# A Fourier basis of a quarter period, enc x spectrum in fp32r parts, and the mixing of tile 0 behind four sums

## The reference, cut to what matters

```python
base = jnp.einsum('bsd,od->bso', x, W_base) + b_base
e0 = jnp.einsum('bsd,rd->bsr', x, enc0)            # rank 32
e1 = jnp.einsum('bsd,rd->bsr', x, enc1)            # rank 8
w0 = coefs0 * mask0; w1 = coefs1 * mask1           # 3 experts
decoded = einsum('bsr,eor->ebso', e0, w0) + einsum('bsr,eor->ebso', e1, w1)
update = real_fourier_orthogonal_multiply(decoded).sum(axis=0)
return base + update * SCALING                     # SCALING = 0.5
...
x = x + L0_ffn(L0_cond(x, itok_B_0_15, L0_cond_weights), ...)
x = x + L1_ffn(L1_cond(x, itok_B_0_30, L1_cond_weights), ...)
```

## Time and profile before

| | us |
|---|---|
| median of 3 runs | 227.8 |
| lowest and highest | 227.55 and 227.83 |
| the profiled execution's own time | 227.68 |
| its span, first to last instruction | 225.5 |

### The profile page before, as it was taken

The page is one execution under the profiler, slowest core; times in us unless marked ns, Lnnn a source line. Parts: engine busy times, 40 slices in busy tenths (PEclk is TensorE's granted clock), DMA queues, the critical chain, the costliest instruction groups (busy, mean ns, idle before and its releaser), DMA issues.

```text
span 225.5 us, 3597 instructions
## 1 busy us (share of the span) xinstructions
PE 220.1 (98%) x1212; PEld 185.2 (82%) x1212; DVE 98.8 (44%) x147; ACT 75.0 (33%) x199; POOL 110.1 (49%) x133
## 2 busy tenths in 40 slices
PE   7799999999999999999999999999999999999995
PEld 2568888888888888888888888888888888888884
DVE  4246444344544343445443444454434444544334
ACT  2067233333322333333223333332233333322211
POOL 4757754355566545445665454456654544522200
PEclk9999999999999999999999999999999999999999
DMA  6931022333222323322233323221232332212112
GB/s 201 310 99 52 9 96 96 102 93 84 72 53 96 99 96 99 99 63 88 52 96 99 96 99 99 71 81 52 96 99 96 99 99 81 73 49 90 47 49 93
DMA packets 13543, 20.42 MB, mean 91 GB/s; under 512 B 2618, under 2 KB 4538, under 8 KB 13538
## 3 DMA queue, kind: packets, MB, share of 16 engines
q1 hardware_dynamic: 10642, 18.16, 25.3%
q0 software_dynamic: 2048, 1.05, 2.4%
q10 hardware_dynamic: 848, 1.14, 1.5%
HBM read 11.96 MB, written 8.39 MB: 90 GB/s over the span
## 4 chain that ended last, share of the span: by engine, by line
PE 95%; DMA 3%; DVE 0%; ACTq 0%; issue 0%
PE f_ps L443 26%; PE y_ps L423 26%; PE f_ps L453 13%; PE f_ps L460 13%; PE f_ps L465 13%; DMA basis_sb<-in_fourier_basis 3%; PE a_ps L481 2%; PE a_ps L408 1%; PE y_ps L417 0%; DVE x L392 0%; PE a_ps L460 0%; PE f_ps L417 0%; PE a_ps L465 0%; ACTq L260 0%; ACTq L259 0%
## 5 line engine op out<-in xcount | busy, mean ns | idle before, releaser
L224 POOL TENSOR_TENSOR x<-x_in,bias 128x512 f32<-128x512 f32 x32 | 40.9, 1278 | 81.0 <-issue 46.9
L217 POOL DMA_INDIRECT gathered<-in_L_cond_weights,row_now x58 | 56.5, 974 | 13.2 <-issue 10.1
L443 PE MATMUL f_ps<-a_high,y_high 128*128 128x512 f32 x128 | 53.8, 420 | 0.0
L443 PE MATMUL f_ps<-a_low,y_high 128*128 128x512 f32 x128 | 50.3, 393 | 0.0
L358 DVE TENSOR_TENSOR x<-f_ps,x 128x512 f32<-128x512 f32 x32 | 22.1, 692 | 49.4 <-PE f_ps L443 47.9
L286 ACT ACTIVATE y_high<-y_ps 128x512 fp32r<-128x512 f32 x32 | 19.1, 597 | 69.6 <-PE y_ps L423 69.6
L282 ACT ACTIVATE y_high<-y_ps 128x512 fp32r<-128x512 f32 x32 | 19.1, 597 | 61.4 <-PE y_ps L423 61.4
L460 PE MATMUL f_ps<-b_sign,y_high 128*128 128x512 f32 x124 | 36.5, 415 | 0.0
L423 PEld LDWEIGHTS y_ps<-blocks,x_in 128*128 128x128 f32 x256 | 33.5, 191 | 3.5 <-issue 0.7
L423 PEld LDWEIGHTS y_ps<-blocks,x 128*128 128x128 f32 x256 | 33.4, 191 | 3.2 <-DVE x L358 0.5
L453 PE MATMUL f_ps<-a_high,y_low 128*128 128x512 f32 x128 | 35.1, 396 | 0.0
(11 more groups left out here) (44 smaller groups left out, 73.0 us busy)
## 6 DMA issues: line engine op xcount, KB each, us to landing
x_in<-in_x SPq DMA_DIRECT2D x31, 256.0 KB, 2.7
out_x<-x SPq DMA_DIRECT2D x31, 256.0 KB, 2.0
gathered<-in_L_cond_weights,row_now POOLq DMA_INDIRECT x58, 2.4
w_sb<-in_L_ffn_W_base SPq DMA_DIRECT2D x1, 512.0 KB, 7.5
w_sb<-in_L_ffn_W_base ACTq DMA_DIRECT2D x1, 512.0 KB, 8.9
basis_sb<-in_fourier_basis SPq DMA_DIRECT2D x1, 257.0 KB, 3.3
basis_sb<-in_fourier_basis ACTq DMA_DIRECT2D x1, 257.0 KB, 6.7
bias<-in_L_ffn_b_base SPq DMA_DIRECT2D x1, 256.0 KB
```

The lines of the kernel that those rows point to most:

```text
L217: nc.gpsimd.indirect_dma_start(gathered[:, slot, layer, :], None, mix_rows[layer], IndirectOffsetOnAxis(rows[:, layer:layer + 1].bitcast(u ...
L224: nc.gpsimd.tensor_tensor(out=x1[:, slot, :], in0=x_in[:, slot, :], in1=bias[:, :], op=ALU.add).then_inc(biased, 1)
L443: last = nc.tensor.matmul(f0_ps[:, :], y0_high[:, k * P:(k + 1) * P], a[:, k, :], start=(k == 0 and a is a_high), stop=(k == CHUNKS - 1 an ...
```

## The change

It does four things.

1. The table holds a quarter of a period (129 columns) in one array of 258 KB instead of two of 257 KB, and only SP loads it. `decode` gets two copies of the 40 ranks side by side (rows 0 to 39 and 64 to 103) and two negated chunks. PE forms four sums of two fp32 matmuls of 129 columns each instead of two sums of two with 257; the second sum of sines waits for the negated chunks. DVE builds `spectrum` from four quarters, some of them read backwards.
2. enc is loaded twice, to partitions 0 to 39 and 64 to 103, from ACT's queue instead of SP's. ACT rounds it to fp32r (`enc_parts`), DVE puts the rest into rows 64 and up. `spectrum` is split into `spectrum_high` and `spectrum_low` too. Per bank one fp32r matmul takes both parts of enc with the high spectrum, and a second one takes enc's high part (64 rows) with the low spectrum, in place of one fp32 matmul.
3. The masks are issued first on ACT's queue, and DVE treats them before `row_of` and before clearing `blocks`.
4. The mixing of tile 0 stands behind all four banks on PE, its `expand` and y0_high behind all four a_high on ACT, and low0(1) behind all a_low on DVE, where the signs are converted before the residual of tile 0. There are 13 warm-up matmuls instead of 18.

The diff, without declarations of semaphores and with shape changes left out:

```diff
+        decode = sb("decode", [P, CHUNKS + 2, 2, ENC_LOW], f32)
         enc_sb = sb("enc_sb", [P, T], f32)
-        odd_part = sb("odd_part", [P, HALF], f32)
-        mirrored = sb("mirrored", [P, HALF], f32)
+        enc_parts = sb("enc_parts", [P, T], f32r)
         constant2 = sb("constant2", [P, 1], f32)
+        sines = sb("sines", [P, 2, QUARTER], f32)
         spectrum = sb("spectrum", [P, T], f32)
+        spectrum_high = sb("spectrum_high", [P, T], f32r)
+        spectrum_low = sb("spectrum_low", [P, T], f32r)
...
+        sine_ps = [sums[:, 0:QUARTER] for sums in (y1_ps, y0_ps)]
+        cosine_ps = [sums[:, 0:QUARTER] for sums in (f1_ps, f0_ps)]
...
-            sp.dma_start(coefs_sb[:, :, :], coefs).then_inc(coefs_loaded, 16)
-            sp.dma_start(basis_sb[:, 1], basis[1]).then_inc(basis_loaded[1], 16)
+            sp.dma_start(coefs_sb[:, :, :, :], coefs).then_inc(coefs_loaded, 16)
+            sp.dma_start(basis_sb[:, :, :], basis).then_inc(basis_loaded, 16)
             load_w(sp, 0)
-            sp.wait_ge(enc_zero, 1)
-            sp.dma_start(enc_sb[0:R, :], enc).then_inc(enc_loaded, 16)
             sp.dma_start(bias[:, :], b_base.partition_broadcast(P)).then_inc(bias_loaded, 16)
...
+            act.dma_start(masks_sb[:, :, :, :], masks).then_inc(masks_loaded, 16)
             act.dma_start(kinds[:, :, :], kinds_in).then_inc(kinds_loaded, 16)
-            act.dma_start(masks_sb[:, :, :], masks).then_inc(masks_loaded, 16)
-            act.dma_start(basis_sb[:, 0], basis[0]).then_inc(basis_loaded[0], 16)
+            act.wait_ge(enc_zero, 1)
+            for first in (0, ENC_LOW):
+                act.dma_start(enc_sb[first:first + R, :], enc).then_inc(enc_loaded, 16)
             load_w(act, 1)
             act.dma_start(x_in[:, 0, :], x_tiles[0]).then_inc(x_loaded[0], 16)
...
-            act.wait_ge(odd_done, 1)
-            nc.scalar.activation(odd_part[:, :], odd_ps, ACT.Copy, scale=SCALING).then_inc(odd_ready, 1)
-            act.wait_ge(blocks_zero, 1)
-            expand(0, 0)
+            def spectrum_side(half):
+                act.wait_ge(quarters_ready, 2 * half + 2)
+                nc.scalar.activation(spectrum_high[:, halves[half]], spectrum[:, halves[half]], ACT.Copy, scale=SCALING
+                                     ).then_inc(spectrum_high_ready, 1)
+            for n in range(2):
+                act.wait_ge(sines_done, n + 1)
+                nc.scalar.activation(sines[:, n, :], sine_ps[n], ACT.Copy).then_inc(sines_ready, 1)
+            act.wait_ge(enc_loaded, 32)
+            nc.scalar.activation(enc_parts[:, :], enc_sb[:, :], ACT.Copy).then_inc(enc_high_ready, 1)
+            spectrum_side(0)
+            spectrum_side(1)
             def high0(count):
                 act.wait_ge(mixed0, count)
                 nc.scalar.activation(y0_high[:, :], y0_ps[:, :], ACT.Copy).then_inc(y0_high_ready, 1)
...
             for k in range(CHUNKS):
-                if k == FIRST_MIX:
-                    high0(1)
                 act.wait_ge(a_done, k + 1)
                 nc.scalar.activation(a_high[:, k, :], a_ps[k][:, :], ACT.Copy).then_inc(a_high_ready, 1)
+            act.wait_ge(blocks_zero, 1)
+            expand(0, 0)
+            high0(1)
             expand(1, 0)
...
-            nc.vector.memset(blocks[:, :, :, :], 0.0).then_inc(blocks_zero, 1)
-            nc.vector.memset(decode[:, :, :], 0.0).then_inc(decode_zero, 1)
+            nc.vector.memset(decode[:, :, :, :], 0.0).then_inc(decode_zero, 1)
             dve.wait_ge(partition_ready, 1)
             nc.vector.tensor_scalar(channel[:, :], partition[:, :], C - 1, None, ALU.bitwise_and).then_inc(channel_ready, 1)
+            dve.wait_ge(coefs_loaded, 16)
+            dve.wait_ge(masks_loaded, 16)
+            nc.vector.tensor_tensor(out=masked[:, :, :, :], in0=coefs_sb[:, :, :, :], in1=masks_sb[:, :, :, :], op=ALU.mult).then_inc(masked_ready, 1)
+            dve.wait_ge(masked_ready, 1)
+            nc.vector.tensor_tensor(out=pair[:, :, :], in0=masked[:, 0, :, :], in1=masked[:, 1, :, :], op=ALU.add).then_inc(pair_ready, 1)
+            dve.wait_ge(pair_ready, 1)
+            dve.wait_ge(decode_zero, 1)
+            for copy in range(2):
+                nc.vector.tensor_tensor(out=decode[:, 0:CHUNKS, copy, 0:R], in0=pair[:, :, :], in1=masked[:, 2, :, :], op=ALU.add).then_inc(decode_ready, 1)
+            dve.wait_ge(decode_ready, 2)
+            nc.vector.tensor_scalar(decode[:, CHUNKS:, :, 0:R], decode[:, 1:3, :, 0:R], -1.0, None, ALU.mult).then_inc(negated, 1)
             dve.wait_ge(channel_ready, 1)
             dve.wait_ge(kinds_loaded, 16)
             nc.vector.tensor_scalar(row_of[:, :, :], kinds[:, :, :], float(C), channel[:, :], ALU.mult, ALU.add).then_inc(row_of_ready, 1)
-            dve.wait_ge(coefs_loaded, 16)
-            dve.wait_ge(masks_loaded, 16)
-            nc.vector.tensor_tensor(out=masked[:, :, :], in0=coefs_sb[:, :, :], in1=masks_sb[:, :, :], op=ALU.mult).then_inc(masked_ready, 1)
-            dve.wait_ge(masked_ready, 1)
-            nc.vector.tensor_tensor(out=pair[:, :], in0=masked[:, 0, :], in1=masked[:, 1, :], op=ALU.add).then_inc(pair_ready, 1)
-            dve.wait_ge(pair_ready, 1)
-            dve.wait_ge(decode_zero, 1)
-            for first, rank, at in ((0, R0, 0), (CHUNKS * R0, R1, R0)):
-                part = slice(first, first + CHUNKS * rank)
-                nc.vector.tensor_tensor(out=decode[:, :, at:at + rank], in0=pair[:, part].rearrange("p (q r) -> p q r", r=rank),
-                                        in1=masked[:, 2, part].rearrange("p (q r) -> p q r", r=rank), op=ALU.add).then_inc(decode_ready, 1)
-            dve.wait_ge(odd_ready, 1)
-            nc.vector.tensor_scalar(constant2[:, :], odd_part[:, 0:1], 2.0, None, ALU.mult).then_inc(constant_ready, 1)
+            nc.vector.memset(blocks[:, :, :, :], 0.0).then_inc(blocks_zero, 1)
+            dve.wait_ge(sines_ready, 1)
+            nc.vector.tensor_scalar(constant2[:, :], sines[:, 0, 0:1], 2.0, None, ALU.mult).then_inc(constant_ready, 1)
             dve.wait_ge(constant_ready, 1)
-            nc.vector.tensor_scalar(mirrored[:, :], odd_part[:, :], -1.0, constant2[:, :], ALU.mult, ALU.add).then_inc(mirrored_ready, 1)
-            dve.wait_ge(mirrored_ready, 1)
-            dve.wait_ge(even_done, 1)
-            nc.vector.scalar_tensor_tensor(out=spectrum[:, 0:HALF], in0=even_ps, scalar=SCALING, in1=odd_part[:, :],
-                                           op0=ALU.mult, op1=ALU.add).then_inc(spectrum_ready, 1)
-            nc.vector.scalar_tensor_tensor(out=spectrum[:, T - 1:HALF - 1:-1], in0=even_ps[:, 1:HALF - 1], scalar=SCALING,
-                                           in1=mirrored[:, 1:HALF - 1], op0=ALU.mult, op1=ALU.add).then_inc(spectrum_ready, 1)
+            dve.wait_ge(cosines_done, 1)
+            nc.vector.tensor_tensor(out=spectrum[:, 0:QUARTER], in0=cosine_ps[0], in1=sines[:, 0, :], op=ALU.add).then_inc(quarters_ready, 1)
+            dve.wait_ge(cosines_done, 2)
+            dve.wait_ge(sines_ready, 2)
+            nc.vector.scalar_tensor_tensor(out=spectrum[:, HALF:QUARTER - 1:-1], in0=cosine_ps[1][:, 0:QUARTER - 1], scalar=constant2[:, :],
+                                           in1=sines[:, 1, 0:QUARTER - 1], op0=ALU.add, op1=ALU.subtract).then_inc(quarters_ready, 1)
+            nc.vector.tensor_tensor(out=spectrum[:, HALF + 1:HALF + QUARTER], in0=cosine_ps[1][:, 1:QUARTER], in1=sines[:, 1, 1:QUARTER],
+                                    op=ALU.add).then_inc(quarters_ready, 1)
+            nc.vector.scalar_tensor_tensor(out=spectrum[:, T - 1:HALF + QUARTER - 1:-1], in0=cosine_ps[0][:, 1:QUARTER - 1], scalar=constant2[:, :],
+                                           in1=sines[:, 0, 1:QUARTER - 1], op0=ALU.add, op1=ALU.subtract).then_inc(quarters_ready, 1)
+            dve.wait_ge(enc_high_ready, 1)
+            nc.vector.tensor_tensor(out=enc_parts[ENC_LOW:, :], in0=enc_sb[ENC_LOW:, :], in1=enc_parts[ENC_LOW:, :].bitcast(f32),
+                                    op=ALU.subtract).then_inc(enc_low_ready, 1)
+            for half, columns in enumerate(halves):
+                dve.wait_ge(spectrum_high_ready, half + 1)
+                nc.vector.scalar_tensor_tensor(out=spectrum_low[:, columns], in0=spectrum[:, columns], scalar=SCALING,
+                                               in1=spectrum_high[:, columns].bitcast(f32), op0=ALU.mult, op1=ALU.subtract
+                                               ).then_inc(spectrum_low_ready, 1)
...
             for k in range(CHUNKS):
-                if k == FIRST_MIX:
-                    low0(1)
                 dve.wait_ge(a_high_ready, k + 1)
                 nc.vector.tensor_tensor(out=a_low[:, k, :], in0=a_ps[k][:, :], in1=a_high[:, k, :].bitcast(f32),
                                         op=ALU.subtract).then_inc(a_low_ready, 1)
-            residual0(0, 1)
+            low0(1)
             dve.wait_ge(bits_loaded, 16)
```

(36 more changed lines are left out.)

40 lines of the change are left out of this document (20 added, 20 removed).

## The result

The change makes the kernel slower: 234.58 us median (231.42 to 236.24, 4 runs) against 227.81 (227.55 to 228.53, 4 runs); the ratio is 1.0215, 95% interval 1.0163 to 1.0267. I had forecast 228.3 with a range of 227.0 to 229.4. The ratio counts the two quicker executions, 231.42 and 234.25, as the other two lie over 1.5% above the quickest. The direction was right, the size was not: the likeliest case was to cost 0.5 us, the change costs 4.9 by the ratio and 6.8 by the medians. The kernel is slower beyond the noise; with this interval and these four executions it isn't settled that it is slower by more than 2%. The profiled execution took 234.25 us, its span is 232.4 where it was 225.5.

The account below looks back on a forecast made before the run. PE, busy 98% of the span, bounds the kernel; its start is bound by a load. F' = 11.50 + 5.86 = 17.36, 0.62 later than before; 227.68 + 0.62 = 228.3 us, range 227.0 to 229.4.

Parts of the forecast that it names:

- The front: Start up to the sums: sums start at 6.0 us instead of 8.49, take 2.0, done at 8.0.
- W_base: Load the transposes wait for: first half stays at 9.17 us, second lands 0.8 earlier, at 10.25.
- E': Start of enc x spectrum in the changed kernel: 11.50 us, 0.71 earlier than before; point of balance 10.88.
- the rival in which that half doesn't move: W_base's second half lands no earlier: E' 12.30, 229.1 us; chance 0.14, shared with 64-row products costing restarts.
- The products: Enc x spectrum on PE: 1.86 us instead of 3.45, 1.6 less; 64-row restarts bounded at 1.1, taken as nothing.
- The tail: Serial chain behind the four banks to the first feed: E' + 5.86, against E + 4.53 before.
- F': Start of the first feed in the changed kernel: E' + 5.86 = 17.36 us, 0.62 later than 16.74.
- The clock: Rival: PE's clock falls in the new idle time before and behind the mixing, + 1.9, 230.2 us; chance 0.08.
- The gathers: POOL's gathers for tile 0 land at 13.96 us, hidden by 0.1; rival that they arrive last: 229.2, chance 0.10.
- the sign conversion: Signs converted before the residual, while PE feeds tile 0: costs nothing.
- the stream: PE's tiles after the first feed: order unchanged, steps of 6.45 us as before.

Follow-up runs that it names:

- e3: Changed kernel with 128 rows in both products and nine dummy matmuls in the wait for W_base: 232.61 us, ratio 1.0178.
- e1: Changed kernel with nine dummy matmuls between the first eight transposes and the wait for W_base's second half: 232.81 us, ratio 1.0229.
- e2: Changed kernel with 128 rows instead of 64 in each bank's second product, no dummies: 230.81 us, ratio 1.0152.
- e12: Changed kernel, 64-row products kept, with nine dummies before the second transposes, seven before the mixing, three behind it: 230.40 us, ratio 1.0139.
- e11: Changed kernel with both loads of enc on SP's queue behind W_base's first half: 233.31 us, ratio 1.0248.
- e6: e3 with eleven more dummies between the last product and the mixing of tile 0, three before the first feed: 230.30 us, ratio 1.0090.
- e7: Kernel before with part 4 of the change alone, 18 warm-ups: 231.43 us, ratio 1.0141.
- e5: e3 with the mixing of tile 0, its expand, y0_high and y0_low put back where they were before: 227.77 us, ratio 0.9994.
- e9: e5 with kinds and row_of first and both loads of enc on SP: 227.13 us, ratio 0.9971.
- e4: Kernel before with 13 warm-ups instead of 18: 228.04 us, ratio 1.0016.
- e8: Kernel before with only enc x spectrum in fp32r, 128 rows in both products, enc loaded twice from SP: 227.22 us, ratio 0.9997.
- e10: e8 with 23 warm-ups instead of 18: 226.94 us, ratio 0.9956.

## Why the prediction was wrong

**The front: right.** The sums started at 5.89 (forecast 6.0) and ended at 7.7 (8.0); `masked` started at 4.06 (4.1). The sums began 2.6 us earlier than before, as I had it, and that is where the kernel's gain ends.

**W_base: right in sum, wrong in its parts.** The first half, which I had left at 9.17, landed 4.8 us after its issue at 1.66, so near 6.5, in this execution (the transposes waited for it until 9.4 in e3, so it scatters by about 3 us). The second half, which I had moved 0.8 forward by counting KB, to 10.25, landed at 10.76, 0.3 forward, and later still in e1, e2 and e12. The step that failed is "The second half has 97 KB less ahead of it on ACT's queue", taken as 0.8 us earlier. It left E' at 11.90, 0.40 late; the first half no longer counted. That is halfway to the rival in which that half doesn't move (12.30). By the rule of the Trainium skill which I quoted there (page "DMA: Bandwidth & Descriptors", section "Why a DMA increments its semaphore by 16 and not by 1"), loads of 40 rows are spread over ten engines only, so that fewer KB ahead save nothing on those ten. A landing at 10.76 and later, not at 10.25, agrees with it. e11 doesn't decide it: moving both loads away brought at least 1.1 us, and their 160 KB at the rates of my sum, 70 to 190 KB/us, would also be 0.8 to 2.3. That it is the ten engines which do it no run here shows.

**The products: the step that failed, in size.** I had bounded the 64-row product at 0 to 1.1 us and taken nothing, "since weight loads in the stream hide under the passes". It was 1.4 even at the full clock (3.23 in e1 against 1.86), and 2.0 at the low one, where 128 rows pass at 0.43 and these at 0.72 (7 x 0.29; the rest of the 5.45 is the low clock itself). The bound was too low because I counted one switch a bank, four in all, and there are seven: each of the eight products but the first follows one with another number of rows.

**The tail: right with slow products, too short with quick ones.** F' = E' + 5.86 was the order's price on paper. e1, whose clock held as far as ACT's y0_high, has 19.03 - 12.25 = 6.8 without the restart of 0.27, so 7.05; taking off the 1.3 us by which its products delayed the fourth a_high leaves 5.75. But where the products were as quick as I had them, in e6, the same way took 6.98, or 7.2 counted like 5.86: the fourth a_high started 3.5 us after the first product, not 1.94, for a reason that stays open (last section). The order's cost alone is shown by e7 (3.3 us by the times, 2.5 in the trace).

**The clock: the step that failed in chance and in price.** I gave it 0.08 "against: the 1.4 us between 7.07 and 8.49 left no slow pass", weighed the two stretches of the tail (1.9 and 0.7 us) and not the wait for W_base that I had forecast myself, and assumed that it comes back in 3.8 us of dense work. The changed kernel has three stretches behind one another (2.1 us before the second transposes, 1.75 before the mixing, 0.69 behind it), and the clock stayed low for 13.6 us. I priced the fall at 1.9; e12 shows 3.7 to 4.2 by the medians, 4.0 by the ends of the first feed. This step carries most of the miss.

**The ledger**, by profiled executions, end of the first feed (before 19.57, changed 26.53): clock 4.03 (to e12's 22.50). The other 2.93: E' at 12.30 in e12 where I needed 10.88 to break even, 1.4; and the way from E' to the end of the feed, 10.2 against 5.86 + 2.83 = 8.7 by my sum, 1.5. In this the slow products are 1.3, of which e6 recovered nothing visible, for another reason (last section). The 4.03 is what keeping PE busy gives back with the slow products in place; e2, with equal rows and no dummies, gives back 3.98, so the split holds for this order of the two remedies only. In the forecast 0.62 stood for all.

**The gathers, the sign conversion, the stream: right.** `expand` did not wait in the changed kernel; it began at 17.86. The gathers landed at 13.6 in e5 (13.96 forecast), 0.4 us before the 14.07 at which my sum would have needed them.

## What to carry to other kernels

Before shortening the front of a start-up, read what lands next: here PE got through its sums 2.6 us earlier, to a load that came 0.3 us sooner, and the time became idle. A serial hand-over between engines can cost twice when PE idles in it, in waiting and in its clock; price it with every idle stretch near it, and compare with a variant in which PE is kept busy. Try equal row counts in successive passes, if zeros or harmless terms can fill the rows: the cheapest of the remedies here, one line, brought 3.8 us by the medians (e2).

## What I had not expected of the hardware

- In passes over 128 and 64 rows in turn, the weights are not loaded under the running pass: 0.43 us for each pass of 512 columns at the full clock (e1, e12) against 0.23 with equal rows (e3, e6), 0.72 against 0.43 at the low one (changed kernel, e2).
- In three kernels ACT's a_high came late, with ACT idle. In e3 bank 0 was done at 13.77 and its a_high started at 15.01:

```profile
13.37 0.40 PE L515 MATMUL a_ps<-spectrum_low,enc_parts 128*128 128x256 f32 x2
...
15.01 2.06 ACT L303 ACTIVATE a_high<-a_ps 128x512 fp32r<-128x512 f32 x4 [5.76 <-PE a_ps L515]
```

In e6 bank 1 was done at 13.47, ACT free at 14.24, and the a_high started at 15.03; in e12 it was 13.82, 14.15 and 14.95. In e1, e2 and the changed kernel the same step followed in 0.03 to 0.25 us. In e6 this ate what the faster products gave. It isn't the dense work of PE alone: in e9, with the same nine dummies, the same quick passes and the clock at 1.00, the first a_high followed its bank in 0.04. What ACT waited for stays open; I tried nothing on it.
- The same kernel falls to the low clock in some executions and not in others: three of ten in e4, two of six in e7 and in e8. None of seven fell in e10, which differs from e8 by 1.1 us of dummies only; with so few executions that may be chance.
- The granted clock of the profile doesn't show the slow warm-ups: it reads 1.00 from 0 to 4 us, where the passes of 512 columns come 0.43 apart. It shows the later falls, and the mean clock of an execution counts these: 0.971 of 232.4 us is 13.5 us at the low level, and the stretches give 13.6.
- The time that lies around the span is shorter with part 2 of the change: 1.76 to 1.95 us in every execution of the changed kernel, e1 to e3, e5, e6 and e8 to e12, against 2.16 to 2.54 in the kernel before, e4 and e7. Of the 1.0 us by which e10 beats the kernel before by the medians, this is 0.4. No trace shows what lies there.
